# Perceiver block: the cross-attentions' output projection for two batches at a time

## The reference

```
q = query @ Wq + bq                      # query = layernorm(x)
kv = context @ Wkv + bkv                 # 16 heads of 16
scores = jnp.einsum('bhid,bhjd->bhij', q, k) * scale
scores = jnp.where(mask[:, None, None, :], -jnp.inf, scores)
attn = jax.nn.softmax(scores, axis=-1)
out = jnp.einsum('bhij,bhjd->bhid', attn, v)
out = out.transpose(0, 2, 1, 3).reshape(b, sq, d)
return out @ Wout + bout                 # and x = x + this
```

## Time and profile before

| | |
|---|---|
| median of three runs | 3038.64 us |
| the profiled execution | 3042.65 us, span 3040.4 us, mean granted TensorE clock 0.956 |
| TensorE busy | 2752.3 us (91% of the span) |
| VectorE busy | 1401.3 us (46%) |
| ScalarE busy | 1071.5 us (35%) |
| GpSimd busy | 478.3 us (16%) |
| first cross-attention | from the start to about 931 us |
| second cross-attention | about 1330 to 2194 us |

### The profile page before, as it was taken

How to read it: one execution, slowest core, us unless ns; L and a number is a source line. 1 busy time by engine, 2 the same in 40 slices (tenths; PEclk the granted TensorE clock), 3 DMA queues, 4 the chain that set the end, 5 groups by cost and what they waited for, 6 DMA issues and landing times. The chain is left out here.

```text
span 3040.4 us, 95394 instructions
## 1 busy us (share of the span) xinstructions
PE 2752.3 (91%) x43460; PEld 1885.8 (62%) x43460; DVE 1401.3 (46%) x2411; ACT 1071.5 (35%) x1480; POOL 478.3 (16%) x406
## 2 busy tenths in 40 slices
PE   6999999999997699988999999999868998897858
PEld 3666666666665566655666666666547777776445
DVE  3444544535445711135545454544445454444268
ACT  2333333333333321123343434434334454543123
POOL 2424233243332000001000000000001111111000
PEclk9999999999997599999999999999979999999869
DMA  2110111101100000130111111110110000000000
GB/s 84 35 35 24 39 29 29 39 25 35 35 2 12 29 28 28 42 107 26 38 29 35 34 35 34 29 40 24 43 36 3 3 4 3 4 3 5 40 31 14
DMA packets 48630, 88.96 MB, mean 29 GB/s; under 512 B 8496, under 2 KB 43120, under 8 KB 46832
## 3 DMA queue, kind: packets, MB, share of 16 engines
q1 hardware_dynamic: 48240, 82.96, 9.1%
HBM read 81.89 MB, written 1.05 MB: 27 GB/s over the span
## 5 line engine op out<-in xcount | busy, mean ns | idle before, releaser
L525 DVE TENSOR_REDUCE x_mx<-banks 128x2 f32<-128x800 f32 (+1 forms) x512 | 507.3, 993 | 305.3 <-PE banks L640 215.9
L726 PE MATMUL banks<-x_wv,x_cT 128*128 128x256 f32 (+1 forms) x1664 | 466.6, 403 | 24.2 <-DVE x_nmb L530 21.1
L584 PE MATMUL banks<-x_cT,x_wk 128*128 128x400 f32 (+1 forms) x1024 | 362.5, 510 | 18.2 <-DMA x_cT<-in_ctx 18.2
L726 PEld LDWEIGHTS banks<-x_wv,x_cT 128*128 128x128 f32 (+1 forms) x1664 | 279.0, 186 | 145.6 <-issue 76.0
L433 ACT ACTIVATE x_PT<-banks,x_kbs 128x1024 f32<-128x1024 f32 (+1 forms) x208 | 231.8, 1114 | 376.8 <-PE banks L692 376.8
L433 ACT ACTIVATE x_PT<-banks 128x1024 f32<-128x1024 f32 (+1 forms) x208 | 213.0, 1024 | 429.8 <-PE banks L692 358.7
L692 PE MATMUL banks<-x_qbd,x_kT 32*128 32x128 f32 x6656 | 294.4, 273 | 0.0
L584 PEld LDWEIGHTS banks<-x_cT,x_wk 128*128 128x128 f32 x1024 | 192.8, 192 | 163.4 <-issue 27.1
L678 PE MATMUL banks<-x_PT,x_V 128*32 128x64 f32 x13312 | 272.1, 222 | 20.7 <-ACT x_PT L433 20.7
L692 PEld LDWEIGHTS banks<-x_qbd,x_kT 32*128 32x128 f32 x6656 | 253.4, 182 | 0.0
L678 PEld LDWEIGHTS banks<-x_PT,x_V 128*32 128x32 f32 x13312 | 204.9, 109 | 73.7 <-ACT x_PT L433 25.8
(11 more groups left out here) (314 smaller groups left out, 3780.2 us busy)
## 6 DMA issues: line engine op xcount, KB each, us to landing
x_cT<-in_ctx SPq DMA_DIRECT2D x96, 400.0 KB, 3.7
x_cT<-in_ctx SPq DMA_DIRECT2D x32, 401.0 KB, 3.6
e_wu<-in_mo_up SPq DMA_DIRECT2D x9, 512.0 KB, 3.8
e_wd<-in_mo_down SPq DMA_DIRECT2D x9, 512.0 KB, 4.6
x_mrow<-in_mask_row SPq DMA_DIRECT2D x1, 3202.0 KB, 11.3
g_w<-in_db_w SPq DMA_DIRECT2D x3, 1024.0 KB, 7.4
d_wqk<-in_db_qk SPq DMA_DIRECT2D x1, 2048.0 KB, 8.1
f_wgu<-in_fp_gu SPq DMA_DIRECT2D x1, 1536.0 KB, 6.2
```

The lines of the kernel that those rows point to most:

```text
L525: dve.reduce_max(mx[:, H0[k]:H0[k] + 3:2, kb], g.PS[:, first:first + 2, 0:KBS[kb]], AXX).then_inc(max_read, 1)
L584: last = pe.matmul(PJ[pb][:, 0:KBS[k]], wk[:, c, gg, :], cT[:, (p + 1) % 2, c, KB0[k]:KB0[k] + KBS[k]], start=c == 0, stop=c == KC - 1)
L726: last = pe.matmul(PJ[pb][0:CHK[c], 0:D], cT[:, p, cc, 128 * c:128 * c + CHK[c]], wv[:, cc, :], start=cc == 0, stop=cc == KC - 1)
```

## The change

The projection now runs once for two batches. `oN` gets a second slot and becomes [128, 4, 2, 64], one slot for each parity. The tail of a body with p = 1 (which finishes an even batch) only does the denominators and writes slot 0. The tail of a body with p = 0 (an odd batch) writes slot 1 and then projects both: four matmuls with 128 stationary columns and 256 moving ones, 128 rows of output, and one addition for the whole tile. The bank is used and counted in these bodies only, and the wait for the bias moves from the first to the second of the early bodies.

```diff
-        oN = sb("oN", [128, 4, S])
+        oN = sb("oN", [128, 4, 2, S])
...
-            def __init__(self, bank, ahead, attend, tail):
+            def __init__(self, bank, p, ahead, attend, tail):
...
-                self.DEN, self.WO = (bank.use(1), bank.use(2)) if tail else (None, None)
+                self.DEN = bank.use(1) if tail else None
+                self.WO = bank.use(2) if tail and not p else None
...
-                    dve.tensor_tensor(oN[:, :, :], oT[:, :, :], rec[:, :].rearrange("p (j q) -> p j q", j=4), ALU.mult)\
+                    dve.tensor_tensor(oN[:, :, 1 - p, :], oT[:, :, :], rec[:, :].rearrange("p (j q) -> p j q", j=4), ALU.mult)\
                        .then_inc(on_done, 1)
...
-                    if not later(b, 2):
+                    if not later(b, 3):
                         dve.wait_ge(bias_out, 2)
-                    tile = i if p else i - 1
-                    x = g.X[64 * (1 - p):64 * (1 - p) + 64, bass.ds(tile, 1), :]
-                    dve.tensor_tensor(x, x, PJ[pb][64 * (1 - p):64 * (1 - p) + 64, None, 0:D], ALU.add)\
+                    x = g.X[:, i - 1:i, :]
+                    dve.tensor_tensor(x, x, PJ[pb][:, None, 0:D], ALU.add)\
                        .then_inc(free[pb], 1)
...
-                    if tail and c == C_WO:
+                    if plan.WO and c == C_WO:
                         add_output()
...
-                    if tail and u in (U_DEN, U_WO):
-                        pb, use = plan.DEN if u == U_DEN else plan.WO
+                    shared = {U_DEN: plan.DEN, U_WO: plan.WO}.get(u)
+                    if shared:
+                        pb, use = shared
                         pe.wait_ge(free[pb], bank.value(pb, use))
...
-                        last = pe.matmul(PJ[pb][64 * (1 - p):64 * (1 - p) + 64, 0:D], oN[:, j, :], wo[:, j, :],
+                        last = pe.matmul(PJ[pb][:, 0:D], oN[:, j, :, :].rearrange("p e q -> p (e q)"), wo[:, j, :],
                                          start=j == 0, stop=j == 3)
```

More of the change, by code:

```diff
@@ L257, in cross_attention @@
             count = Bank()
-            SECT.append((kinds, [Schedule(count, *k) for k in kinds], tuple(used), tuple(count.local)))
+            SECT.append((kinds, [Schedule(count, p, *k) for p, k in enumerate(kinds)], tuple(used), tuple(count.local)))
             used = [u + steps * x for u, x in zip(used, count.local)]
```

## The result

The changed kernel takes 3004.59 us (median of 4 runs, 2998.62 to 3013.75), the kernel before 3040.35 us beside it (median of 4). The ratio is 0.9882, 95% interval 0.9853 to 0.9911: 1.2% faster. The forecast was 3005.5 us, 3001 to 3014.

A forecast was written before the change was run, and what follows sets the result against it. TensorE was taken to bound both cross-attentions (768.00 of 790 us busy in the first); 30.6 + 2.5 = 33.1 us off the median of 3038.64 us gave 3005.5 us, range 3001 to 3014.

The forecast's parts named there:

- The groups removed: Output projection in bodies with p = 1, both attentions: 16 groups go, 1.91 us of TensorE each, 30.6 us off.
- The groups that stay: Bodies with p = 0: the 128-column step takes 3.38 us against 3.56, 0.18 less, 14 times, 2.5 us off.
- rival of exposed loads: Remaining projection groups: wide weight loads cost 53 ns more per record, so only 23.8 us off, 3014.8 us; chance 0.10.
- Waits in place of the work: Shortened step: TensorE idles for chunk 5's exp or chunk 6's maximum, 27.2 us lost, 3032.7 us; chance 0.05.
- The additions: VectorE: 16 residual additions go with their waits; nothing on TensorE waits for them, so counted as nothing.
- The slower rival: VectorE's gapped multiply delays V's copy in chunk 3; break-even 1.1 us each, as slow as reciprocal 3045.5 us; chance 0.02.

The follow-up runs named there:

- width experiment: Against the kernel before: the group on 128 columns but still issued in every body, half of each projection thrown away; 3035.89 us, ratio 0.9973.
- second profile of the changed kernel: The changed kernel measured once more, unaltered, against the kernel before; 3005.24 us, ratio 0.9876.
- two-additions kernel: The changed kernel with the residual addition of a tile split into two halves of 64 partitions; 3011.39 us in one run.
- control: The changed kernel, one multiply, with GpSimd's four products per batch in the first attention cut to 64 of 1024 columns; 3014.44 us in one run.

## Why the prediction was right, by its steps

*The groups removed:* 1.91 us each was forecast. Odd batches went from 55.2 to 53.3 us and from 52.2 to 50.3, 1.91 us in either attention, seven times each. The eighth, b = 15, had the same price: from its value matmuls to the next V projection 2.46 us before and 0.58 after.

*The groups that stay:* the step was forecast at 3.38 us and is 3.42. The early load of V came as built from the neighbours (197.24 against 197.45), the start of the group 0.06 us later (0.65 us, not 0.59). The prediction had borrowed the 0.59 us from the denominators' matmul; both the narrow and the wide group start 0.65 us after the value matmuls. So 0.14 us for each by the step, 0.15 by the batches, in place of 0.18. The rival of exposed loads is refuted by the 379 ns and by the width experiment. The Trainium skill's rule that a change of tiling mode drains TensorE ("TensorEngine Tiling (Array Packing)", Key Properties) fits: with the wide group there is one change fewer, and the V load is early. No run here isolates it.

*Waits in place of the work:* none came. Over each whole attention TensorE waits 16 times for the exp and 16 times for the correction in both kernels, in the first for 9.6 and 8.7 us.

*The additions:* free, as the odd batches show. The next maximum needs the bank that the addition frees, but the addition ends at 198.08 and the maximum's matmul starts at 198.41, 0.96 us after the V projection, as behind the denominators (0.96): no wait.

*The sum:* 33.1 us was forecast and the attentions gave 35.0. The parts that the change touches gave 32.5: 30.4 for the removed groups (30.6 forecast) and 2.1 for those that stay (2.5 forecast); in the second profile of the changed kernel they gave 32.4. The other 2.5 us are chance. The group after the first attention's last batch has the same 2.40 us of waiting before it, but ran at a granted clock of 1.00 this time and not 0.57, 1.97 us against 3.32, which with what follows it gives 1.4:

```profile
910.13 1.97 PE L664 MATMUL banks<-x_wo,x_oN 128*128 128x256 f32 x8 [2.40 <-DVE x_oN L509]
```

In the second attention its like took 3.56 us (0.2 us more for that end than before), and in the second profile of the same kernel 3.75 in the first. The remaining 1.4 us lie in the first interval of the second attention, 54.1 us before and 52.7 after, where no tail runs. The kernel before waited there 1.34 us for a maximum, once; the two-additions kernel waited 1.14 us for a maximum in the same interval, and the others had only the wait of 0.12 us that all have.

*The time:* the mechanism was right, but that the median came within 0.9 us of the forecast is luck. The forecast set out from 3038.64 us, the kernel before had 3040.35 beside the changed one, and the two medians lie 35.8 us apart (37.7 in the second comparison), with intervals of 6 to 9 us to either side; the four runs of the changed kernel spread over 15.

*The slower rival:* its mechanism is real and its price was wrong. The prediction took each tenth on the multiply as a tenth on TensorE and set the break-even at 1.1 us for each. That holds in the second attention (0.4 to 0.5 us for 0.43). In the first, 0.43 us of work too much cost some 3.9 us, since the instruction then runs into GpSimd's next product. The sign was in the rows: a mean of 521 ns for work that takes 424. That mean mixes three cases in the kernel before: fourteen multiplies of 468 to 489 ns, one of 1184 ns (batch 15) and one of 426. The fourteen and the long one each begin within a product of GpSimd and end 0.28 us after that product's end; the last has no product beside it. The view of the whole program has the longest:

```profile
L508 DVE TENSOR_TENSOR x_oN<-x_oT,x_rec x32: 424/426/1184, 136.8 to 2189.7; 128x256 f32<-128x256 f32 x32
```

The gapped write itself costs nothing (424 to 428 ns in the control).

The Trainium skill, "SBUF — State Buffer", section "SBUF: two separate sides", says that VectorE and GpSimd share a pair of ports as an exclusive lock, which a VectorE instruction with two inputs in SBUF needs against a GpSimd one that reads SBUF. The 2.45 us, against 425 ns without the products, and the end 0.28 us behind the product's agree with it.

## What to carry to other kernels

Where an engine is busy for 97% of a stage, price a removed group from start to start, against a place in the same trace that lacks it: batch 0 gave 1.65 us, and the changed kernel had 1.66. The float32 matmuls with 64 stationary columns here wasted half the array only while they stood alone: two tiles' worth side by side, as one wide matmul or in turn on the two column halves, took the time of one. Before slack on another engine is called free, look at what the instruction would run into: 0.43 us more cost 0.4 us in one attention and 3.9 in the other. And judge a change of 1% by the intervals inside the changed stage, since the untouched stages moved by 17 us between executions here.

## What the runs showed that I had not expected

- Float32 matmuls on columns 0 to 63 and 64 to 127 overlap: 16 records in 1.88 us in turn, 2.76 us one half after the other, against 1.84 for 8 alone. Why the second order overlaps only in part is open.
- A VectorE multiply with both inputs in SBUF that started 0.36 us into a GpSimd product of 2.4 us took 2.45 us in place of 0.43, in 15 of the first attention's 16 tails; the copies out of PSUM that lay within such products kept their 0.42.
- After the same wait of 2.40 us the same group runs at the full clock in one execution (1.97 us) and at the lower one in another (3.75). What decides it is open.
